# A decoder layer on one core: two PSUM banks for row maxima and three for scores, a paired third-tile exp, and outputs handed on by halves

## What is computed

```python
x = _layernorm(x + _L0_attn_ref(x, ...))          # scores, causal mask, softmax, values, out_w
x = _layernorm(x + _L0_xattn_ref(x, ctx_1024, ...))
x = _layernorm(x + _L0_ffn_ref(x, wg, w1, w3, w2)) # router, top 2 of 8 experts, silu(h1) * h3, w2

scores = jnp.einsum('bhqd,bhkd->bhqk', qh, kh) / jnp.sqrt(jnp.float32(hd))
scores = jnp.where(causal, scores, jnp.float32(-jnp.inf))
attn = jax.nn.softmax(scores, axis=-1)
o = jnp.einsum('bhqk,bhkd->bqhd', attn, vh).reshape(b, m, d)
return o @ out_w.T + out_b
```

## Time and profile before

| what | value |
|---|---|
| median of 3 runs | 249.91 us (249.85 to 252.05) |
| the profiled execution's own time | 248.22 us |
| its span, first to last instruction | 246.4 us |
| granted TensorE clock, mean | 0.997 |
| busy: PE, DVE, ACT, POOL | 232.7, 186.0, 161.3, 89.1 us |
| exps of the attention (line 1348) | 136, of which 32 have 256 columns |

### The profile page before, as it was taken

How to read it: one execution, slowest core, us unless ns; L and a number is a source line. 1 busy time by engine, 2 the same in 40 slices (tenths; PEclk the granted TensorE clock), 3 DMA queues, 4 the chain that set the end, 5 groups by cost and what they waited for, 6 DMA issues and landing times.

```text
span 246.4 us, 4685 instructions
## 1 busy us (share of the span) xinstructions
PE 232.7 (94%) x1438; PEld 164.7 (67%) x1438; DVE 186.0 (75%) x631; ACT 161.3 (65%) x332; POOL 89.1 (36%) x161
## 2 busy tenths in 40 slices
PE   7999999999999999999999999988899999999981
PEld 3456668666666776677765576553588878987860
DVE  5558987989879899986876898990399763348974
ACT  2488785889778779897898734747368765022234
POOL 9998547241432453355221211174011000470300
PEclk9999999999999999999999999999999999999998
DMA  6990002000003100000221000011311101010101
GB/s 237 340 330 3 1 1 85 3 1 4 0 0 117 56 1 3 1 0 3 81 87 60 32 1 3 0 53 58 106 32 44 45 21 54 25 53 11 39 7 43
DMA packets 10568, 12.57 MB, mean 51 GB/s; under 512 B 1200, under 2 KB 7728, under 8 KB 10416
## 3 DMA queue, kind: packets, MB, share of 16 engines
q1 hardware_dynamic: 9456, 10.43, 12.9%
q0 software_dynamic: 512, 1.05, 1.4%
q10 hardware_dynamic: 576, 0.79, 0.9%
HBM read 9.25 MB, written 3.01 MB: 50 GB/s over the span
## 4 chain that ended last, share of the span: by engine, by line
PE 80%; DVE 10%; ACT 4%; issue 3%; DMA 2%; DVEq 0%; ACTq 0%; SPq 0%
PE psB L1083 12%; PE psA L1054 12%; PE psO L1106 10%; PE psJ L952 3%; PE psJ L1186 3%; PE psJ L990 3%; PE psJ L953 3%; PE psJ L1067 2%; PE psA L1249 2%; PE psO L1111 2%; PE psO L982 2%; PE psJ L1065 2%; PE psA L1231 2%; PE psJ L997 1%; DMA xT<-xt_dram 1%
## 5 line engine op out<-in xcount | busy, mean ns | idle before, releaser
L1576 DVE CUSTOM_DVE_ANT_0 junk<-psA,c 128x128 bf16<-128x128 f32 (+3 forms) x128 | 55.7, 487 | 8.8 <-PE psA L1054 8.4
L1348 ACT ACTIVATE prob<-psB 128x512 f32<-128x512 f32 (+1 forms) x88 | 47.4, 558 | 13.6 <-PE psB L1083 11.8
L1083 PE MATMUL psB<-qb,kst 128*128 128x512 f32 (+3 forms) x128 | 38.0, 338 | 0.2 <-ACT prob_more L1348 0.2
L1054 PE MATMUL psA<-kst,qa 128*128 128x512 f32 (+1 forms) x88 | 36.6, 425 | 0.0
L1083 PEld LDWEIGHTS psB<-qb,kst 128*128 128x128 f32 x128 | 22.8, 189 | 11.4 <-issue 4.3
L1581 DVE TENSOR_REDUCE negm<-psA 128x3 f32<-128x462 f32 (+1 forms) x48 | 26.4, 579 | 4.5 <-PE psA L1054 3.9
L1348 ACT ACTIVATE prob_more<-psB 128x512 f32<-128x512 f32 (+1 forms) x48 | 24.5, 527 | 6.1 <-PE psB L1083 5.9
L1392 ACT ACTIVATE silu<-psA 128x512 f32<-128x512 f32 x16 | 9.6, 599 | 24.4 <-DVE hid L1739 18.0
L899 POOL TENSOR_SCALAR_AFFINE_SELECT prob<-prob 128x256 f32<-128x256 f32 x32 | 13.0, 408 | 31.3 <-ACT prob_more L1348 31.3
L1054 PEld LDWEIGHTS psA<-kst,qa 128*128 128x128 f32 x88 | 16.4, 188 | 6.0 <-issue 3.9
L1106 PE MATMUL psO<-prob_more,v 128*32 128x512 f32 (+3 forms) x128 | 20.3, 439 | 0.0
(11 more groups left out here) (198 smaller groups left out, 562.6 us busy)
## 6 DMA issues: line engine op xcount, KB each, us to landing
c<-w_dram SPq DMA_DIRECT2D x8, 256.0 KB, 2.6
w<-w_dram SPq DMA_DIRECT2D x1, 1024.0 KB, 4.7
xs_dram<-kst SPq DMA_DIRECT2D x1, 960.0 KB, 7.2
ys_dram<-ys SPq DMA_DIRECT2D x7, 128.0 KB, 1.8
rest<-xs_dram SPq DMA_DIRECT2D x3, 256.0 KB, 2.8
c<-c_dram SPq DMA_DIRECT2D x1, 666.0 KB, 8.5
xT<-xt_dram SPq DMA_DIRECT2D x2, 256.0 KB, 4.7
x_tok<-x_dram SPq DMA_DIRECT2D x1, 512.0 KB, 9.5
```

What stands on the lines that cost most here:

```text
L1054: last = nc.tensor.matmul(ps[:, c:c + heads * width].rearrange("p (n w) -> p n w", n=heads), qa[:, u % SLOTS, 128 * i:128 * i + 128], keys ...
L1083: last = nc.tensor.matmul(ps[:, c:c + S - 128 * kt], keys, qb[:, u % 2, 128 * kt:S], start=m == 0, stop=m == len(blocks) - 1, skip_group_c ...
L1348: nc.scalar.activation(dst, psB[n % SIZE["B"]][:, 0:cols], ACT.Exp, scale=SCALE).then_inc(b_done[n % SIZE["B"]], 1)
L1576: last = nc.vector.tensor_tensor_reduce(out=junk[:, p, cols], in0=psA[p][:, cols], in1=c32[:, C_MASK + S - width:C_MASK + S], scale=-1.0, ...
```

## The change

1. `SIZE` gives the ring of row maxima two banks and the ring of scores three. `psA`, `psB`, `junk` and the semaphores follow from it.
2. In stage 0 the third key tile of two heads shares one bank and one exp (two runs of 256 columns): 10 B fills per unit instead of 12.
3. The second pair of outputs of a batch row (p odd) is transposed and divided by halves: `OT` becomes two jobs of two blocks, with `ONT` of each half waiting for its own. For these pairs VectorE's reciprocal covers 16 sums instead of 32 and each product half the columns, and there are twice as many of both. The planner is told of it.
4. `EARLY` is another table, so the order of the work changes on all engines.
5. VectorE's `CQ` waits in addition for the `low` part of the earlier piece (a semaphore).

```diff
-SIZE = {"A": 3, "B": 2, "O": 1, "J": 2}
+SIZE = {"A": 2, "B": 3, "O": 1, "J": 2}
...
-        kinds = (((0, 0),), ((1, 0), (3, S - 128)), ((2, 0),))
-        return [tuple((kt, j, c) for kt, c in tiles) for tiles in kinds for j in range(G)]
+        kinds = (((0, 0),), ((1, 0), (3, S - 128)))
+        return [tuple((kt, j, c) for kt, c in tiles) for tiles in kinds for j in range(G)] + [((2, j, 0), (2, j + 1, 256)) for j in range(0, G, 2)]
...
-        return {0: range(4), 1: range(4, 8), 3: range(4, 8), 2: range(8, 12)}[kt]
+        return {0: range(4), 1: range(4, 8), 3: range(4, 8), 2: range(8, 10)}[kt]
...
+def turns(p):
+
+    return [("OT", (p, h)) for h in range(2)] if p % 2 else [("OT", (p,))]
...
-            add("ONT", (st, b, h), [("PE", 0.24), ("ACT", 0.3)], [("OT", (p,))],
+            add("ONT", (st, b, h), [("PE", 0.24), ("ACT", 0.3)], [("OT", (p, h)), ("OT", (p - 1,))],
...
-    ('A', 11): 2, ('A', 13): 11, ('A', 14): -6, ('A', 7): -28, ('A', 8): 284, ('B', 1): 194, ('B', 13): 61, ('B', 6): 38,
+    ('A', 11): -121, ('A', 12): -28, ('A', 13): -15, ('A', 3): 39, ('A', 4): 30, ('A', 9): 8, ('B', 0): -77, ('B', 1): 556,
...
-                    for i in range(QT):
+                    for i in range(QT) if len(args) == 1 else (2 * args[1], 2 * args[1] + 1):
                         last = nc.tensor.transpose(ps[:, 128 * i:128 * i + 128], po_sb[:, 128 * i:128 * i + 128], ident)
...
-                    job_done(pe, "OT", NG // 2 * (2 * st + b + 1) - 1)
+                    job_done(pe, "OT", NG // 2 * (2 * st + b + 1) - 2)
+                    job_done(pe, "OT", NG // 2 * (2 * st + b + 1) - 1, h)
...
+                    scores = psB[n % SIZE["B"]][:, :]
+                    if st == 0 and kt == 2:
+
+                        dst = (prob, prob_more)[j // 2][:, u % 2, :].rearrange("p (j c) -> p j c", j=2)[:, :, 1024:1280]
+                        scores = scores.rearrange("p (j c) -> p j c", j=2)
...
-                    nc.scalar.activation(dst, psB[n % SIZE["B"]][:, 0:cols], ACT.Exp, scale=SCALE).then_inc(b_done[n % SIZE["B"]], 1)
+                    nc.scalar.activation(dst, scores, ACT.Exp, scale=SCALE).then_inc(b_done[n % SIZE["B"]], 1)
...
+                    tiles = slice(0, QT) if len(args) == 1 else slice(2 * args[1], 2 * args[1] + 2)
+                    n = tiles.stop - tiles.start
...
+                    link(nc.vector.reciprocal(rec[:, p % 2, at], ps[:, :].rearrange("p (n c) -> p n c", c=V_AT)[:, at, HD]))
...
                     dve.wait_ge(s_hi, pieces(PART["x", b])[0])
+
+                    dve.wait_ge(s_lo, pieces(PART["x", b])[0] - PART["c",])
```

More of the change, by code:

```diff
@@ L266, in tasks @@
         p = u // 2
-        add("POC", (p,), [("ACT", 0.49)], [last_pv(u)] + ([(("OT", (p - 1,)), 0)] if p else []))
-        add("OT", (p,), [("PE", 0.44), ("DVE", 0.8)], [("POC", (p,)), ("LOAD", (3,))],
-            [(1, ("ONT", row(u - NG) + (1,)))] if g == 1 and u >= NG else [])
+        add("POC", (p,), [("ACT", 0.49)], [last_pv(u)] + ([(turns(p - 1)[-1], 0)] if p else []))
+        for item in turns(p):
+            whole = len(item[1]) == 1
+            add("OT", item[1], [("PE", 0.44), ("DVE", 0.8)] if whole else [("PE", 0.24), ("DVE", 0.5)], [("POC", (p,)), ("LOAD", (3,))],
+                [(1, ("ONT", row(u - NG) + (1,)))] if g == 1 and u >= NG else [])
         if g < NG - 1:
@@ L1115, in _ @@
                 elif kind == "OT":
-                    p, = args
+                    p = args[0]
                     loaded(s_id, 16)
@@ L1341, in _ @@
                     kt, j, _ = b_fills(u)[k][0]
[L1342 to L1345, removed]
-                    else:
-                        cols, dst = S, prob_at(u, kt, j)
-                    nc.scalar.activation(dst, psB[n % SIZE["B"]][:, 0:cols], ACT.Exp, scale=SCALE).then_inc(b_done[n % SIZE["B"]], 1)
+                    scores = psB[n % SIZE["B"]][:, :]
+                    if st == 0 and kt == 2:
+                        dst = (prob, prob_more)[j // 2][:, u % 2, :].rearrange("p (j c) -> p j c", j=2)[:, :, 1024:1280]
+                        scores = scores.rearrange("p (j c) -> p j c", j=2)
+                    elif st == 0:
+                        half, first = (prob, prob_more)[j // 2], j % 2 * 1280 + [0, 512][kt]
+                        dst = half[:, u % 2, first:first + S]
+                    else:
+                        dst = prob_at(u, kt, j)
+                    nc.scalar.activation(dst, scores, ACT.Exp, scale=SCALE).then_inc(b_done[n % SIZE["B"]], 1)
                 elif kind == "POC":
@@ L1352, in _ @@
                     if p:
-                        job_filled(act, ("OT", (p - 1,)))
+                        for other in turns(p - 1):
+                            job_filled(act, other)
                     nc.scalar.activation(po_sb[:, :], psO[:, :], ACT.Copy).then_inc(s_po, 1)
@@ L1585, in _ @@
                 elif kind == "OT":
-                    p, = args
+                    p = args[0]
                     ps = bank(JOB[item])
                     if p % 2 == 0 and p:
[L1589 to L1592, removed]
+                        for h in range(2):
+                            job_filled(dve, ("ONT", divmod(p // 2 - 1, 2) + (h,)))
+                    tiles = slice(0, QT) if len(args) == 1 else slice(2 * args[1], 2 * args[1] + 2)
+                    n = tiles.stop - tiles.start
+                    o = ps[:, :].rearrange("p (i j h c) -> p i j h c", i=QT, j=G, h=2)[:, tiles]
+                    at = slice(2 * G * tiles.start, 2 * G * tiles.stop)
+                    link(nc.vector.reciprocal(rec[:, p % 2, at], ps[:, :].rearrange("p (n c) -> p n c", c=V_AT)[:, at, HD]))
+                    sums = rec[:, p % 2, at].rearrange("p (i j h) -> p i j h", i=n, j=G)
                     for h in range(2):
                         first = 32 * (p * 2 % NG + h)
-                        ins = nc.vector.tensor_tensor(onorm[:, :, first:first + 32].rearrange("p i (j d) -> p i j d", j=G), o[:, :, :, h, 0:HD],
-                                                      sums[:, :, :, h].unsqueeze(3).to_broadcast([128, QT, G, HD]), ALU.mult)
+                        ins = nc.vector.tensor_tensor(onorm[:, tiles, first:first + 32].rearrange("p i (j d) -> p i j d", j=G), o[:, :, :, h, 0:HD],
+                                                      sums[:, :, :, h].unsqueeze(3).to_broadcast([128, n, G, HD]), ALU.mult)
                     free(JOB[item], ins)
```

## The result

The changed kernel takes 260.12 us (median of 4 runs, 259.71 to 260.70) beside 250.98 us (249.85 to 252.13) of the kernel before in the same set (a set is what ran together): ratio 1.038, 95% interval 1.033 to 1.043. The forecast was 247.5 us with a range up to 252.5. The profiled execution took 260.70 us, its span is 259.0, 12.6 more than before.

The account below looks back on a forecast made before the run. TensorE was taken as the bound, with some 36 us of waits, exposed weight loads and warm-up matmuls to move. -2.1 + 1.4 - 1.4 - 0.3 = -2.4 us took the median 249.91 to 247.5 us, range 243.5 to 252.5.

Parts of the forecast that it names:

- The banks (-2.1): Attention's score and maxima rings: short refill spacings fall from 14.1 to 10.9 us, two-thirds counted, -2.1 us.
- The expert stage (+1.4): R1, R3 and F1 on two A banks: refills come short, +1.4 us, bounds 0 and +4.2.
- The routing (-1.4): Router's counts 2.9 us earlier, routed tokens' transposes 3.5 earlier, 2.1 us of attention work moved behind: -1.4 us.
- The small parts (-0.3): Paired exps, halved OT, twelve more warm-up matmuls and the CQ wait: together -0.3 us, bounds -1 and +2.
- The sum: Whole kernel: banks, expert stage, routing and small parts add to -2.4 us, giving 247.5 us.
- VectorE runs dry: Rival, stage-0 value bursts: two A banks leave VectorE too few full banks, maxima come late; +2.9, 252.8 us; chance 0.20.
- The mark that I gave for it: Attention: VectorE's 8.4 us wait for psA doubles and stage-0 units take over 10 us each.
- The other mark: Routing: the forecast is wrong if the router's counts are not earlier; they were expected near 153 us.
- All of it arrives: Rival, attention: two thirds of B's 9.2 us gained, A's waits hidden under the exps; 242.4 us; chance 0.07.
- it evens out: Rival: A's 6.0 us cancel 5 to 6 of B's 9.2, experts cancel routing; 249.8 us; chance 0.27.
- The clock falls: Rival: tighter A ring drops TensorE to 1.2 GHz between counts and transposes, 13 us more; 262 us; chance 0.02.

Follow-up runs that it names:

- a third bank alone: Changed kernel, own order, with psO joining the A ring as a third bank from the second row's cross-attention outputs on: 258.09 us, ratio 1.027.
- the fitted kernel: Kernel before with the paired exps alone, three A and two B banks, and EARLY refitted on all ends of the plan: 249.22 us, ratio 0.993.
- the first with whole `OT`: Changed kernel in its own order with OT of pairs 1, 3, 5 and 7 whole again: 255.87 us beside 248.06, ratio 1.031.
- the last set: Changed kernel rerun, 259.92 us (ratio 1.033), together with its order with every OT whole, 261.35 us (1.041), beside the kernel before at 251.63.
- the one with added matmuls: Changed kernel with 32 more warm-up matmuls between the router's counts and the routed tokens' transposes: 260.92 us beside 251.31, ratio 1.041.
- the second with whole `OT`: Changed kernel's order with every OT whole, run again in one set with the changed kernel: 261.35 us beside 251.63, ratio 1.041.

## Why the prediction was wrong

**The banks (-2.1), the step that failed.** "For its price I went through TensorE's order": the count compared spacings with the time a bank is away, and I put 1.3 us for a whole-bank maximum: the time from the fill's start until a free reader begins, the reader's own time, and the hand-back. A bank is away from its fill's start until its reader has ended, and the reader has a queue. Taken for every A fill of the attention of the kernel before, from its first matmul to the end of its last maximum, that is 1.88 us on average, over 2 us for 32% of them. For scores it is 1.28, near the 1.18 I used. The two maxima of the earlier trace rows show it: they begin at 65.94 and 66.55, and their fills are the second and third here (the first was read before them):

```profile
63.49 0.47 PE L1054 MATMUL psA<-kst,qa 128*128 128x512 f32 x1
...
64.50 0.39 PE L1054 MATMUL psA<-kst,qa 128*128 128x512 f32 x1
...
64.95 0.40 PE L1054 MATMUL psA<-kst,qa 128*128 128x512 f32 x1
```

64.50 to 66.63 is 2.1 us. Counted again with these times, 0.1 us for the hand-back and the recorded distances of the old order, 69 refills come too early by 39 us with two A banks, where the three of before had 7 by 0.2. My count for the old order with two A banks was 16.3 us, both rings together. Two thirds of 39 are 26; measured are 34.3 - 12.7 = 21.6 us outside the expert stage (from two sets). This count was made after the result and is rough: without the hand-back it says 33 us, and part of the time away is lead that three banks allow; with two, in the changed kernel, the average is 1.56 us. The ring that showed few waits was not loose. It was just long enough: the rows of waits told which ring hurts today, not how much slack the other has.

**The expert stage (+1.4), the same step.** For R1 the 2.5 us were right (2.43 on average in the kernel before). What I had not looked at is F1: its bank is away 3.85 us on average, since ScalarE may not write `silu` before VectorE has used the one two blocks back. The kernel before: F1(6) on TensorE, its reader on ScalarE, and that reader's row in the list of waits:

```profile
209.12 0.39 PE L946 MATMUL psA<-x_high,wp 128*128 128x512 f32 x1
...
214.04 0.60 ACT L1392 ACTIVATE silu<-psA 128x512 f32<-128x512 f32 x1 [4.80 <-DVE hid L1739]
...
ACT silu L1392 <- DVE hid L1739: 18.0, 9, 4.8
```

5.5 us for one bank, and 18.0 us of waits that I passed over as idle time of an engine that is no bound. Idle time of a reader that leaves a full bank standing is not free. The count with these times says 30 early refills by 18.2 us; measured 12.7 in the old order, past my bound of 4.2, and 5 to 7 in the new one, of which a third bank alone gives 2 back.

**The routing (-1.4).** The counts came 0.6 to 2.2 us later, not 2.9 earlier. TensorE's waits for maxima ahead of them can account for that; no run isolates it. The expected 3.5 us at the transposes did not come either: undisturbed, the distance is 17.9 us against 17.6.

**The small parts (-0.3).** Right in size: pairs 0 in the old order, halves 0 or a small gain in the new one; both in the old one +2.6, 0.6 past my bound of +2. The pairs gain, if at all, only in an order made for them: the 0.7% of the fitted kernel are theirs and its table's together.

**The sum.** The undisturbed profile (the first with whole `OT`) gives +2.2 up to the counts, +0.3 to the transposes, +5.3 in the expert stage: 7.8, what its medians say. Banks, routing and small parts together were forecast at -3.8 and gave +2.5; the expert stage was forecast at +1.4 and gave +5.3. The 1.3 us up to the result's +9.1 are within what the sets differ by; the late starts below are a likely place for them. The range was also narrower than its terms: their bounds, added, reach from -13.7 to +12.2 us, that is from 236 to 262, and the "244.5 to 250" that I gave as its own bounds follow from no sum of them.

**The rivals.** "VectorE runs dry" had the right sign and the right ring. It took the price from the cover lost in bursts, +2.9 in sum, and no more than 1.4 for the experts. The mark that I gave for it failed too: the units kept their pace (from the start of unit 3's to that of unit 4's transposes 9.7 us), and VectorE's wait rose to 11.5, not to double. The other mark, counts that are not earlier, came true. "All of it arrives" and "it evens out" fell with the result. "The clock falls" happened, contrary to the trace of before, but over 6.8 us and not over the routing's 13, which costs 3.4 us at most. The Trainium skill (TensorE: Matmul & The Clock Gate, "A second HAM failure mode: psum-queue depth-cycling") tells of a kernel in which such cycling through banks made the clock fall and rise. The runs here show falls, but don't tie them to the short ring. The kernel with the parts and two A banks in the old order, where TensorE waits most, lost the clock twice in its profile, for 3.4 us from 112.7 us and from 184.4:

```profile
PEclk9999999999999999899999999979999999999999
```

That is 3.4 us of its 37, and the one execution of it that kept the clock at 0.998 still took 283.2 us. Two A banks alone kept the clock in four of five executions, at +34 us, while the kernel before itself, with three, runs at 0.989 to 0.991 in eight of 11 executions of the last set, and the fitted kernel with three A banks and pairs lost the clock for 3.4 us in its profile.

## What to carry to other kernels

Before taking a bank from a ring, measure for every fill how long its bank is away, from the first matmul to the end of its last reader, queue included, and set that against the distance to the fill one bank nearer; few waits in a ring say nothing of the slack that is left. Here such a count overstated the loss, since part of the time away is only lead. Go through every stage that uses the ring, and look for readers that are themselves held back by a double buffer. An order fitted by numbers belongs to one split: compare splits with the tables empty or both fitted anew, on all ends of the program.

## What was not expected of the hardware

In 13 of the 14 profiles of the sets in which the kernel before takes 251 us, and in none of the five of the sets in which it takes 248 (nor in the one of before shown ahead of the prediction), VectorE or ScalarE starts 0.8 to 2.9 us late on matmuls that the trace shows as done, between 165 and 175 us, around the last of GpSimd's scatters. The changed kernel:

```profile
167.29 0.47 PE L1061 MATMUL psA<-kc,qa 128*128 128x462 f32 x1
167.60 0.40 PE L1090 MATMUL psB<-qb,kc 128*128 128x512 f32 x1
...
169.41 1.39 DVE L1594 TENSOR_REDUCE negm<-psA 128x3 f32<-128x462 f32 x2 [2.36 <-PE psA L1061]
...
170.18 0.60 ACT L1360 ACTIVATE prob<-psB 128x512 f32<-128x512 f32 x1 [2.97 <-remote]
...
170.10 0.34 PE L1061 MATMUL psA<-kc,qa 128*128 128x154 f32 x1 [1.03 <-DVE negm L1594]
...
172.30 1.08 PE L1128 MATMUL psJ<-c,po_sb 128*128 128x128 f32 x4 [1.36 <-ACT po_sb L1367]
```

The maximum of the fill at 167.29 starts 1.6 us after its end, the exp of the one at 167.60 2.2 us after its end. TensorE then waits for both, and the half clock begins at 171.7. The times of matmuls in a trace are modelled, so I can't say whether they or their signals were late; the cause stays open. The late start also stands where the added matmuls kept the clock up. It comes ahead of the clock's fall and not from it. It comes again in the expert stage, just behind the last of GpSimd's gathers: a `silu` and a `hid` product both start 1.9 to 2.0 us after their matmuls at 236 to 238 us in the two profiles of the changed kernel, the one with added matmuls and the second with whole `OT`, and not in the first with whole `OT`. The same kernel takes 73.0 us in that stage in the second and 71.5 in the first.
